# Later keys of causal small attentions zeroed by GpSimd after the exponent, with weighing one step on

## The reference

```python
causal = jnp.where(jnp.tril(jnp.ones((S, S), dtype=bool)), 0.0, -1e+30).astype(jnp.float32)
s1 = jnp.einsum('bhqd,bhkd->bhqk', q1, k1) * scale + causal
...
a1 = jax.nn.softmax(s1.astype(jnp.float32), axis=-1).astype(q1.dtype)
...
scores = jnp.where(causal[None, None], scores, jnp.finfo(scores.dtype).min)
probs = jax.nn.softmax(scores, axis=-1)
out = jnp.einsum('bhqk,bkhd->bqhd', probs, v).reshape(b, s, H)
```

## Time and profile before

| | |
|---|---|
| median of 3 runs | 2820.78 us (2817.78 to 2826.1) |
| the profiled execution's own time | 2820.77 us |
| its span | 2819.4 us |
| PE busy | 2135.3 us (76%) |
| DVE busy | 1581.9 us (56%) |
| ACT busy | 1107.2 us (39%) |
| POOL busy | 898.0 us (32%) |
| mean granted clock of TensorE | 0.848 |

### The profile page before, as it was taken

The page is one execution under the profiler, slowest core; times in us unless marked ns, Lnnn a source line. Parts: engine busy times, 40 slices in busy tenths (PEclk is TensorE's granted clock), DMA queues, the critical chain, the costliest instruction groups (busy, mean ns, idle before and its releaser), DMA issues. The chain is left out here.

```text
span 2819.4 us, 35939 instructions
## 1 busy us (share of the span) xinstructions
PE 2135.3 (76%) x13065; PEld 1487.7 (53%) x13112; DVE 1581.9 (56%) x3073; ACT 1107.2 (39%) x2234; POOL 898.0 (32%) x808
## 2 busy tenths in 40 slices
PE   5667635999956888847344999978999968887755
PEld 2333314777645777834212554446888845554444
DVE  6877674444444555545787444443556554355566
ACT  3255415545523444411372244442444434312534
POOL 2867402655536656642251000001233211000002
PEclk9666767999978999978666888998999988899887
DMA  4322100000014444410101000001000000010000
GB/s 132 76 54 62 31 21 28 18 22 11 9 36 149 158 155 157 154 52 1 45 0 37 2 3 3 3 28 71 1 1 1 1 1 2 2 39 7 3 36 15
DMA packets 48431, 114.60 MB, mean 41 GB/s; under 512 B 5472, under 2 KB 18144, under 8 KB 46976
## 3 DMA queue, kind: packets, MB, share of 16 engines
q1 hardware_dynamic: 46720, 108.10, 11.9%
q0 software_dynamic: 1536, 4.20, 0.5%
HBM read 100.09 MB, written 11.14 MB: 39 GB/s over the span
## 5 line engine op out<-in xcount | busy, mean ns | idle before, releaser
L1703 POOL TENSOR_SCALAR l0f_probs<-l0f_probs,l0f_tot 128x128 f32<-128x128 f32 (+1 forms) x256 | 190.3, 762 | 133.0 <-DVE l0f_tot L1657 132.9
L1925 PE MATMUL ps<-l0f_xh,l0f_wh 128*128 128x256 f32 x480 | 148.0, 308 | 49.7 <-DVE l1x_dBu L594 28.3
L1197 DVE TENSOR_REDUCE l2a_a_max<-ps 128x6 f32<-128x768 f32 x128 | 119.4, 955 | 114.2 <-PE ps L1049 113.5
L2875 POOL TENSOR_TENSOR l2x_probs<-l2x_probs,l2x_rc 128x512 f32<-128x512 f32 x64 | 66.5, 1040 | 265.2 <-DVE l2x_rc L2790 265.2
L2040 POOL TENSOR_TENSOR l0f_wl<-l0f_raw,l0f_wh 128x1024 fp32r<-128x1024 f32 x60 | 141.8, 2375 | 17.5 <-ACT l0f_wh L1965 17.5
L1927 PE MATMUL ps<-l0f_xh,l0f_wl 128*128 128x256 f32 x480 | 139.7, 291 | 0.0
L1926 PE MATMUL ps<-l0f_xl,l0f_wh 128*128 128x256 f32 x480 | 139.6, 291 | 0.0
L1587 ACT ACTIVATE l0f_probs<-ps,l0f_neg 128x128 f32<-128x128 f32 (+1 forms) x256 | 104.4, 424 | 87.4 <-DVE l0f_neg L1647 87.4
L1925 PEld LDWEIGHTS ps<-l0f_xh,l0f_wh 128*128 128x128 f32 x480 | 95.5, 199 | 57.5 <-issue 31.8
L619 POOL TENSOR_TENSOR l1x_y<-l1x_y,l1x_hc 128x512 f32<-128x512 f32 x64 | 80.7, 1282 | 126.4 <-DVE l1x_hc L610 126.4
L2731 ACT ACTIVATE l2x_probs<-ps,l2x_neg,l2x_rs 128x256 f32<-128x256 f32 x128 | 71.1, 559 | 123.2 <-DVE l2x_neg L2780 123.2
(11 more groups left out here) (758 smaller groups left out, 5933.5 us busy)
## 6 DMA issues: line engine op xcount, KB each, us to landing
l0f_raw<-in_e_l0f SPq DMA_DIRECT2D x60, 512.0 KB, 3.8
l0x_bc<-scratch_bc SPq DMA_DIRECT2D x32, 512.0 KB, 4.8
l0f_raw_d<-in_e_l0f SPq DMA_DIRECT2D x60, 256.0 KB, 3.7
scratch_rows<-zero SPq DMA_DIRECT2D x1, 3840.0 KB, 18.9
l0f_xb<-scratch_rows SPq DMA_DIRECT2D x15, 256.0 KB, 4.3
scratch_results<-l0f_yb SPq DMA_DIRECT2D x15, 256.0 KB, 4.5
l0f_slab<-in_g_l0f SPq DMA_DIRECT2D x8, 448.0 KB, 3.4
l1f_raw<-in_w_l1f SPq DMA_DIRECT2D x1, 3072.0 KB, 10.0
```

Of the source, the lines that this page charges most:

```text
L1197: dve.tensor_reduce(M[:, 2 * half:2 * half + 2, j, :], src.rearrange("p a (c n) -> p a c n", c=NB_), AX.X, ALU.max).then_inc(*unit_max.tick())
L1703: last = pool.tensor_scalar(pr[:, u % 3, a, r], pr[:, u % 3, a, r], tot[:, u % 3, qt, a:a + 1], None, ALU.mult)
L1925: pe.matmul(out, hi, xh[:, j % 2, c, :], start=c == 0, stop=False)
```

## The change

For causal calls (`late` = 1) three things change. The mask products are left out of `score`. POOL sets the exponents of later keys to zero in `PT`, by two `affine_select` per step (`mask`, L1256 of the new kernel), 128x256 elements each, or 128x512 where `p is None`; `weigh` waits for the new signal `masked` instead of `weighed`. And weigh, copy_out, back and normalise have a lag one step longer. The row maxima still come from masked units, so the exponent of a later key can exceed 1 before it is set to zero.

```diff
+    late = 1 if causal and not scan else 0
+    WEIGH, BACK = 1 + late, 2 + late
...
-        others += [("weigh", O, 0) for O in octet_at(n, 1)] + [("back", O, 0) for O in octet_at(n, 2)]
+        others += [("weigh", O, 0) for O in octet_at(n, WEIGH)] + [("back", O, 0) for O in octet_at(n, BACK)]
...
-                                         QT[z][r, js[i]:js[i] + step, q0:q0 + w], start=i == 0, stop=not causal and i + step == len(js))
-                if causal:
+                                         QT[z][r, js[i]:js[i] + step, q0:q0 + w], start=i == 0, stop=(late or not causal) and i + step == len(js))
+                if causal and not late:
...
-                pe.wait_ge(*weighed(SPO * (O + 1)))
+                pe.wait_ge(*(masked if late else weighed)(SPO * (O + 1)))
...
         def at_pool():
+            def mask(n):
+                O, (kt, p) = n // SPO, hs.parts[n % SPO]
+                pool.wait_ge(*weighed(n + 1))
+                m = 4 if p is None else 2
+                for a in range(2):
+                    part = PT[:, O % 2, a, 1, :, P:S] if p is None else PT[:, O % 2, a, kt, 2 * p:2 * p + 2, 0:P]
+                    last = pool.affine_select(part, part, [[0, m], [1, P]], ALU.is_ge, 0.0, base=0, channel_multiplier=-1)
+                last.then_inc(*masked.tick())
+
             for it, s in STEPS:
+                if late and (it - 2) * NC + s - LEAD >= 0:
+                    mask((it - 2) * NC + s - LEAD)
                 if it < NB2 and s < 2:
```

More of the change, by code:

```diff
@@ L943, in small_attention @@
     unit_ps, unit_max, joined, max_turned, max_taken = k.sig("unit_ps"), k.sig("unit_max"), k.sig("max_joined"), k.sig("max_turned"), k.sig("max_taken")
-    rows = k.sig("max_rows", 16)
+    rows, masked = k.sig("max_rows", 16), k.sig("masked")
     scored, weighed, product, copied, backed, normed = k.sig("scored"), k.sig("weighed"), k.sig("product"), k.sig("out_copied"), k.sig("out_back"), k.sig("out_normed")
@@ L1120, in at_pe @@
                         turn_rows(it - 1)
-                for O in octet_at(n, 1):
+                for O in octet_at(n, WEIGH):
                     weigh(O)
-                for O in octet_at(n, 2):
+                for O in octet_at(n, BACK):
                     back(O)
             for n in TAIL:
-                for O in octet_at(n, 1):
+                for O in octet_at(n, WEIGH):
                     weigh(O)
-                for O in octet_at(n, 2):
+                for O in octet_at(n, BACK):
                     back(O)
```

## The result

The changed kernel takes **2781.45 us** (median of 4 runs, 2778.58 to 2792.75). Before took 2822.86 us on the same chip (2817.78 to 2826.1), so the ratio is 0.9855, 95% interval 0.9828 to 0.9882: 41 us, 1.45%, faster. The forecast was 2795 with a range of 2778 to 2815; rival A had 2787. The same kernel in a second set of runs (e0_change_again) gave 2783.89 us.

The account below looks back on a forecast made before the run. PE was taken as the bound. Unit phase −31.1, drain 0, ends +4.0, shared port +3.6 and later weighing −2 sum to −25.5 us, from 2820.78 to about 2795 us, range 2778 to 2815.

Parts of the forecast that it names:

- rival A: POOL's selects are as cheap as a copy, so ACT paces the drain at 3.7 us: 2787 us, chance 0.27.
- What leaves PE: In l2a and l2f, 120 steps lose two mask products each, 43.2 us of PE time in all.
- What comes through in the unit phase: While units are made, 34.9 us leave PE; 3.8 only filled waits before turned maxima, so −31.1 us come through.
- PE does not wait longer: In a two-unit step PE needs 1.93 us and DVE 1.91, so PE yet waits no longer: no charge.
- may wait for a maximum as it did: The turning back, now behind the units of steps 0, 3, 6 and 9, waits as before: 0 us.
- What POOL gets: 240 in-place selects at 0.6 us for 256 elements and 1.0 for 512, 4.4 us per octet, covered except in the drain.
- The drain: After the last unit, the slowest engine, POOL at 4.4 us per octet, replaces PE at 4.35: gain 0.
- SP is not touched: SP's queue, which issues transfers, was taken as unaffected by the change: no charge.
- The end: At each call's end two long selects stand between last exponent and last weigh: +2.0 us each, +4.0 in all.
- The shared port: In steps 0 and 1 POOL's short selects hold up DVE's low parts, 12 × 0.3 us: +3.6 us.
- Weighing one step on: In step 1, next scores and one more unit go ahead of weigh's wait for the ring, five batches: −2 us.
- Rival D: PE, with less work and more short waits, gets a lower clock: up to 41 us lost, 2815 at half; chance 0.11.

Follow-up runs that it names:

- e0_change_again, e0: The change itself, unaltered, measured once more in a second set of runs: 2783.89 us, ratio 0.9868.
- e4: The change with the mask products kept on PE as well, selects and later lag as they are: 2829.77 us, ratio 1.0029.
- e1: The kernel before with only weighing and turning back one step later, mask products kept, no selects: 2826.43 us, ratio 1.0011.
- e6: The change with DVE's low part issued after the maxima of the same step, not before them: 2770.08 us, ratio 0.9812.
- e7: The change with DVE's row maxima in causal calls taken over half of the keys of each block: 2786.35 us, ratio 0.9874.
- e10: The kernel before with only DVE's low parts moved after the maxima; mask products and old lag kept, no selects: 2804.87 us, ratio 0.993.
- e8: The change with half of the last batch's row transfers issued by ACT's queue, the rest by SP: 2789.52 us, ratio 0.9882.
- e3: The change without its selects, so nothing masks the probabilities and later keys are weighed too: 2799.32 us, ratio 0.9912.
- e2: The change with the old lags: selects on POOL, no mask products, weigh not moved a step later: 2799.05 us, ratio 0.9918.
- e11: The change with DVE's low parts after the maxima and without selects, so later keys are weighed too: 2767.29 us, ratio 0.9785.
- e9: The change with low parts after the maxima, plus two 512-column products on fixed data before three steps' scores per l2a batch: 2779.57 us, ratio 0.9838.

## Why the prediction was right, and where its terms were off

Direction and range were right; the middle, 2795, was 14 us too slow, and rival A, at 2787, was the nearer: its premise came true.

- **What leaves PE (43.2 us): right.** e4 against the change has the same 78.6 us at the lower level in l2a and differs in the products alone: l2a 339.0 − 302.1 = 36.9 us, priced 32 octets × 1.08 = 34.6. In l2f it is 3.4 us (6.2 against e0), priced 8.6, but there e4 has 6.8 us at the lower level, the change 17.1 and e0 9.7. In the medians it is 46 us.
- **What comes through in the unit phase (−31.1): too small, by 7.7 us against before.** Measured −32.3 − 6.5 = −38.8. Some of it is the clock of the one profile of before: its longest batch of l2f took 25.9 us with 10.2 us at the lower level, and in e1 and e4, which keep the products, 21.9 us with 3.4. In l2a the comparison is clean: e1, with the same 64.9 us at the lower level, takes 268.9 us for the seven batches and the change 236.4, −32.5 for a price of 27 octets × 1.08 = 29.2. Per batch the −32.3 and −6.5 are 4.6 and 2.2 us, and the price per batch was 8 × 0.32 + 4 × 0.44 = 4.3, and 2.2. The 3.8 us that I set off for masks that only fill a wait in front of the turned maxima did not show in the sum. The wait there did grow (L1063, 3.6 to 5.8 us), but something else gave as much back. The price was read at full clock, and at the lower level a pair costs more (0.83 us for a pair of 512, from 1700.37 to the next start at 1701.20 in before, against 0.44); whether that is all of it, the runs don't tell.
- **PE does not wait longer: wrong.** The waits for maxima went from 13.6 to 26.3 us. I had balanced the throughput of PE (1.93) and DVE (1.91) in a step, and missed that DVE stands in front of the low part for ACT in steps 0 and 1: 13.8 us for the keys' and 6.7 for the queries' between the first and the last joined maxima of l2a, where before had 6.6 and 2.7. I had also put the turning back behind the units at 0, "may wait for a maximum as it did". It waited 3.2 us before, a row that the prediction's list of the largest waits leaves out, though it is larger than the 2.7 us named there, 8.8 us with the later lag alone (e1) and 12.0 in the change. e6 and e7 price this at 12 us, e10 the part that before already had at 6.
- **What POOL gets (0.6 and 1.0 us): too dear.** 0.41 and 0.64. The Trainium skill's figure (GPSIMD Engine Reference, "Performance pitfalls for Q7 kernels"), from which I had estimated 0.44 to 0.87 us for 512 elements, holds the measured 0.64. The lesson of the forecast is its choice between ends: COPY was the nearest row and I left it for "arithmetic on top".
- **The drain (0): the step held, its size did not.** The slowest of three engines sets the pace, as written, but it is ACT with 3.57 us in place of 4.35, which gives the −5 us of rival A. l2f shows 0.9 to 2.1 us of it. In l2a 1.9 us went into what I had put at nothing, "SP is not touched": PE arrives earlier, the row transfers don't, and the wait for them grew from 0.46 to 2.36 us. The rest is the clock, 10.2 us at the lower level where before had none, some 3.6 us by the estimate; e0 had 3.4 there, so it varies between two executions of the same kernel. e8 shows that these transfers can't be moved to ACT for free.
- **The end (+2.0 each): about 0.7 too much each.** The last weigh starts 1.34 us after the exponent.
- **The shared port (+3.6): 1.4 us** by the lengths, (0.14 + 0.11) × 5 + 0.2, over the same batches. Its indirect part is in the 12 us above: without selects (e3) the waits for maxima are 4.7 us less, and l2a at equal clock 2.2.
- **Weighing one step on (−2): not as argued.** e1 shows none of it (+3 us). e2 shows what it is for: 7 us in the drains, where it keeps the selects off weigh's path, though in l2a longer batches take its 3.4 back. A step's worth depended on another part of the change, and I had costed it on its own.
- **Rival D, the clock: not the net result, but underrated.** The mean over l2a moved by 0.02 only. e3 (0.79), e7 (0.82) and e10 (0.95) show that edits of a few microseconds move it by up to 0.10, that is up to 21 us. The Trainium skill's rule (TensorE: Matmul & The Clock Gate, "The HAM clock gate"), by which less work on PE can cost clock, fits e3 (0.79 over l2a), but e11 has as little work and kept 0.88. That the change came out near before's clock was not something the profile of before could promise: that part of the hit is luck.

## What to carry to other kernels

An operation that can be done anywhere between two steps should go to the engine that idles, and its consumer should be moved one step on with it; the move has no worth on its own but decides whether the slow engine is seen. After relieving the bound, look at what its partner's queue holds in front of the result it owes: here two short instructions in the wrong place cost 12 us beside a gain of 41. Compare variants per stage and with the clock's time at the lower level taken out, because a few microseconds of waits less can be hidden by fifty at the lower level, and the other way round.

## What the runs showed of the hardware that was not expected

- The granted clock of TensorE can stay at the lower level through a whole batch in which PE is hardly ever idle: 0.56 over 46 us with PE busy 43.71 us (e3), 0.69 over 38 us with 36.75 (e6). The next batch, with the same work, can have 1.00. The batches that go low differ from kernel to kernel (the third and fourth of the seven in e3, the second in e7 and e9, the fourth and sixth in e6), while the two profiles of the change have the same stretches all through l2a's unit phase. What picks them stays open.
- A microsecond at the lower level (1.2 GHz) costs about 0.35 us here, by the windows of e6 (an estimate), although PE is busy over 90% of the time.
- An in-place select of POOL on f32 costs what its copy costs: 0.41 us for 128x256, 0.64 for 128x512.
- Four small transfers issued by ACT hold it for 3.60 us; eight on SP take 5.54.
